# A selective-scan kernel: the first tap of its depthwise convolution on ScalarE instead of VectorE

## The reference, cut to what matters

```python
xr = x @ W_in
x_in, res = jnp.split(xr, 2, axis=-1)
xc = jnp.transpose(x_in, (0, 2, 1))
xc = lax.conv_general_dilated(xc, conv_w, (1,), [(d_conv - 1, 0)], feature_group_count=d_inner)
xc = xc + conv_b[None, :, None]
u = jax.nn.silu(jnp.transpose(xc, (0, 2, 1)))
...
def step(h, inp):
    u_t, d_t, B_t, C_t = inp
    h = jnp.exp(d_t[..., None] * A) * h + (d_t * u_t)[..., None] * B_t[:, None, :]
    y = jnp.einsum('bds,bs->bd', h, C_t)
    return (h, y)
...
y = y * jax.nn.silu(res)
return y @ W_out
```

## Time and profile before

| | before |
|---|---|
| median of three runs | 2191.8 us (2189.04 to 2195.35) |
| the profiled execution | 2192.7 us, of which span 2190.9 us |
| PE busy | 2052.0 us (94%) |
| DVE busy | 1500.5 us (68%) |
| POOL busy | 1484.7 us (68%) |
| ACT busy | 1450.1 us (66%) |
| largest shares of the last chain | PE 55%, DVE 15%, ACT 14% |

### The profile page before, as it was taken

One profiled execution on the slowest core, in us unless ns is written; L12 is line 12 of the kernel. 1 busy time (PEld: TensorE's weight loads), 2 busy tenths in 40 slices (PEclk: granted clock), 3 DMA queues, 4 the chain that ended last, 5 costly groups with the idle time before them and its releaser, 6 DMA issues.

```text
span 2190.9 us, 30857 instructions
## 1 busy us (share of the span) xinstructions
PE 2052.0 (94%) x11952; PEld 1444.5 (66%) x11952; DVE 1500.5 (68%) x1507; ACT 1450.1 (66%) x2294; POOL 1484.7 (68%) x845
## 2 busy tenths in 40 slices
PE   6989899999999999999999999999999889999997
PEld 3457677777777777777676777777777764444443
DVE  1268888888897989797879888887888970111201
ACT  0278888898887888888878888888788731000000
POOL 0039897989898888989897979798889960000000
PEclk9989999999999999999999999999999999989999
DMA  5211111111111112111111121111111410000000
GB/s 182 88 58 40 58 41 60 40 60 49 60 39 59 39 60 68 41 68 39 61 41 58 41 68 40 60 42 66 40 50 39 155 59 37 1 29 0 10 0 19
DMA packets 34137, 113.13 MB, mean 52 GB/s; under 512 B 6148, under 2 KB 8836, under 8 KB 33480
## 3 DMA queue, kind: packets, MB, share of 16 engines
q1 hardware_dynamic: 33992, 111.17, 14.9%
HBM read 95.95 MB, written 15.20 MB: 51 GB/s over the span
## 4 chain that ended last, share of the span: by engine, by line
PE 55%; DVE 15%; ACT 14%; issue 11%; POOL 4%; DMA 1%; SPq 0%; DVEq 0%; POOLq 0%; ACTq 0%
PE b_ps L1107 11%; PE y_all L1118 9%; DVE hid L855 8%; ACT hid L545 6%; ACT dub_t L558 5%; PE y_all L1216 5%; PE b_ps L1216 4%; DVE u L730 4%; PE bank_b L999 3%; POOL hid L418 3%; PE bank_a L1014 3%; PE y_all L919 3%; PE bank_b L1014 2%; PE bank_a L1023 2%; PE y_all L1229 2%
## 5 line engine op out<-in xcount | busy, mean ns | idle before, releaser
L855 DVE TENSOR_TENSOR_SCAN hid<-hid,b_ps 128x512 f32<-128x512 f32 x1024 | 1213.5, 1209 | 247.6 <-PE b_ps L1107 225.9
L418 POOL TENSOR_TENSOR hid<-hid,c_rep 128x1024 f32<-128x1024 f32 x512 | 1208.3, 2388 | 200.1 <-DVE hid L855 200.1
L1107 PEld LDWEIGHTS b_ps<-ident,dub_t 128*128 128x128 f32 x4096 | 481.8, 143 | 389.3 <-issue 220.1
L1107 PE MATMUL b_ps<-ident,dub_t 128*128 128x128 f32 x4096 | 637.8, 279 | 71.2 <-DVE hid L855 67.1
L545 ACT ACTIVATE hid<-delta,neg_a 128x512 f32<-128x512 f32 x1024 | 652.9, 711 | 0.4
L1118 PE MATMUL y_all<-ident,hid 128*128 128x128 f32 x4096 | 619.9, 275 | 7.3 <-POOL hid L418 6.3
L558 ACT ACTIVATE dub_t<-du_t,b_t 128x512 f32<-128x512 f32 x768 | 490.3, 712 | 58.9 <-PE b_ps L1107 57.2
L1118 PEld LDWEIGHTS y_all<-ident,hid 128*128 128x128 f32 x4096 | 484.1, 142 | 11.1 <-POOL hid L418 11.1
L409 POOL TENSOR_SCALAR dub_t<-du_t,b_t 128x512 f32<-128x512 f32 x256 | 174.7, 710 | 0.0
L730 DVE SCALAR_TENSOR_TENSOR u<-bank_b,conv_w_sb,u 128x511 f32<-128x511 f32 (+2 forms) x192 | 139.3, 725 | 0.7
L999 PE MATMUL bank_b<-xn,w_in_sb 128*128 128x512 f32 x256 | 132.1, 602 | 3.3 <-DVE u L730 3.3
(11 more groups left out here) (190 smaller groups left out, 1783.2 us busy)
## 6 DMA issues: line engine op xcount, KB each, us to landing
c_rep<-bc_dram SPq DMA_DIRECT2D x128, 512.0 KB, 3.7
hid<-x_t SPq DMA_DIRECT2D x4, 2048.0 KB, 8.7
x_dram<-x_out SPq DMA_DIRECT2D x16, 512.0 KB, 2.9
xt<-x_dram SPq DMA_DIRECT2D x15, 512.0 KB, 3.7
h_dram<-hid SPq DMA_DIRECT2D x4, 512.0 KB, 3.3
out<-y_d SPq DMA_DIRECT2D x4, 512.0 KB, 2.6
x_dram<-hid SPq DMA_DIRECT2D x3, 512.0 KB, 2.7
c_rep<-x_dram SPq DMA_DIRECT2D x3, 512.0 KB, 5.1
```

The source lines that it names most:

```text
L418: nc.gpsimd.tensor_tensor(part, part, c_rep[:, n % 2, s % GROUP, :].unsqueeze(1) .broadcast_to([P, HALF, SEQ]), ALU.mult).then_inc(hc_read ...
L855: nc.vector.tensor_tensor_scan(hid[:, i % RING, d, :], hid[:, i % RING, d, :], b_ps[d % 2][:, :], 0.0, ALU.mult, ALU.add)\
L1107: last = nc.tensor.transpose(b_ps[d % 2][:, c * P:(c + 1) * P], dub_t[:, i % DUB, c, d * P:(d + 1) * P], ident[:, :])
```

## The change

Tap 0 leaves DVE. ACT makes it with one activation (Identity, scale and bias each a column of 128 values) from `bank_b`, behind the same two waits that DVE had. In ACT's program it stands behind `decay` of s = 10, 12 and 14 for tiles 0, 1, 2 of block k+2, and behind `decay` of s = 0 of the next iteration for tile 3. DVE keeps taps 1 to 3 at their steps, and they still count on `conv[m]`.

```diff
+                    def first_tap(k, m):
+                        act.wait_ge(x_done, NI * k + m + 1)
+                        if k >= 2:
+                            act.wait_ge(skip_done, NI * (k - 2) + m + 1)
+                        nc.scalar.activation(u[:, k % 2, m, :], bank_b[:, :], ACT.Identity, scale=conv_w_sb[:, m, CONV - 1:CONV],
+                                             bias=vec_sb[:, 0, m:m + 1]).then_inc(conv[m], 1)
+
...
                             if live(k):
                                 decay(k, s)
+                            if s in (10, 12, 14) and live(k + 2):
+                                first_tap(k + 2, (s - 10) // 2)
+                            if s == 0 and live(k + 1):
+                                first_tap(k + 1, NI - 1)
...
                     def tap(k, m, t):
-                        if t == 0:
-                            dve.wait_ge(x_done, NI * k + m + 1)
-                            if k >= 2:
-                                dve.wait_ge(skip_done, NI * (k - 2) + m + 1)
-                            nc.vector.tensor_scalar(u[:, k % 2, m, :], bank_b[:, :], conv_w_sb[:, m, CONV - 1:CONV],
-                                                    vec_sb[:, 0, m:m + 1], ALU.mult, ALU.add).then_inc(conv[m], 1)
...
-                    TAP_AT = {(9, 2): (0, 0), (9, 3): (0, 1), (10, 0): (0, 2), (10, 1): (0, 3),
...
+                    TAP_AT = {(9, 3): (0, 1), (10, 0): (0, 2), (10, 1): (0, 3),
```

More of the change, by code:

```diff
@@ L720, in tap @@
                     def tap(k, m, t):
-                        if t == 0:
-                            dve.wait_ge(x_done, NI * k + m + 1)
-                            if k >= 2:
-                                dve.wait_ge(skip_done, NI * (k - 2) + m + 1)
-                            nc.vector.tensor_scalar(u[:, k % 2, m, :], bank_b[:, :], conv_w_sb[:, m, CONV - 1:CONV],
-                                                    vec_sb[:, 0, m:m + 1], ALU.mult, ALU.add).then_inc(conv[m], 1)
[L727 to L731, removed]
+                        w = CONV - 1 - t
+                        dve.wait_ge(conv[m], CONV * k + t)
+                        nc.vector.scalar_tensor_tensor(u[:, k % 2, m, t:], bank_b[:, 0:SEQ - t], conv_w_sb[:, m, w:w + 1],
+                                                       u[:, k % 2, m, t:], ALU.mult, ALU.add).then_inc(conv[m], 1)
                     def b_copy(k):
@@ L744, in gating @@
                                                 gate_t[:, k % 2, :, dc * P:(dc + 1) * P], ALU.mult).then_inc(gated, 1)
-                    TAP_AT = {(9, 2): (0, 0), (9, 3): (0, 1), (10, 0): (0, 2), (10, 1): (0, 3),
[3 rows of a table removed]
+                    TAP_AT = {(9, 3): (0, 1), (10, 0): (0, 2), (10, 1): (0, 3),
+                              (11, 3): (1, 1), (12, 0): (1, 2), (12, 1): (1, 3),
+                              (13, 3): (2, 1), (14, 0): (2, 2), (14, 1): (2, 3),
+                              (15, 3): (3, 1)}
                     LATE_TAP_AT = {(0, 0): (3, 2), (0, 1): (3, 3)}
```

## The result

| | before | after |
|---|---|---|
| median | 2191.5 us (4 runs, 2189.0 to 2195.4) | 2249.0 us (4 runs, 2241.0 to 2252.4) |
| ratio, 95% interval | | 1.0256 (1.0223 to 1.0288) |
| the profiled execution | 2192.7 us, span 2190.9 | 2251.4 us, span 2249.6 |
| mean granted TensorE clock | 0.977 of full speed | 0.961 |

Slower, as predicted, but by 57.5 us where 20 were forecast and 32 was the end of the range. The prediction's mechanism is in the trace; so is something else, more than half of the loss, that it had waved through.

What follows compares the result with a forecast made beforehand. It took waits between evenly loaded engines as the bound, chiefly PE waiting for ACT's gate at s = 4. 1.35 us for each of 15 iterations, 20.2 us, gave 2212.0 us; range 2197 to 2224, 8 in 10.

Steps and rivals of the forecast that it cites:

- The mechanism: ACT, running in order, waits at first taps for `in_x` and holds up what follows; 1.35 us per iteration lost.
- its four places: First taps of tiles 0 to 3 on ACT, with idle times near 2.7, 3.7, 1.5 and 1.6 us.
- Rival 1: The gain as meant: ACT's spare time hides the added passes, 19 us gained, 2173 us; chance 0.07.
- Rival 2: Tile 3's delay holds, copies held at (9,2), (11,2), (12,2) are absorbed: -0.14 us per iteration, 2190 us; chance 0.09.
- The sum: From gate to gate, 1.35 us lost per iteration, over 15 iterations 20.2 us.
- steps A to C: Tiles 0 to 2: late taps hold copies that PE waits for, leaving tile 3's `in_x` 0.34 us late.
- step D: Tile 3's tap: `times_b` 1 starts 3.97 us late against 2.3 us spare; gate 0 ends 1.35 us late.
- A: Tile 0's tap delays `y_copy` 3, holding PE's `du_turn` 0 by 0.6 us; 0.53 gained becomes 0.13 lost.
- C: At (12,2), `out_x` waits for `du_copy` 3; behind DVE's three taps PE is 0.45 us late.
- B: Tile 1's tap delays `du_copy` 2, holding PE's `du_turn` 3; the scan of (11,3) starts 0.30 us late.
- I take these to cancel: First iteration: smaller loss at tile 0 without `y_copy`, against tile 3's tap coming later in warm-up; no net size.
- One iteration stands for all: Iteration 8 was read for all; they repeat to hundredths of a microsecond, apart from the first and last two.

Runs made afterwards that it cites:

- e5: The changed kernel with all four first taps moved later in ACT's order, to where ACT reaches them after PE's bank is full: 2186.6 us, ratio 0.9973.
- e1: The changed kernel with tile 3's first tap given back to DVE, tiles 0, 1, 2 staying on ACT: 2219.5 us, ratio 1.0134.
- e2: The kernel before with only tile 3's first tap moved to ACT: 2221.5 us, ratio 1.0141.
- e12: The changed kernel with 18 extra 128-column transposes among PE's narrow products and 16 at the gate: 2237.3 us, ratio 1.0205 to the kernel before.
- e11: The kernel before with 18 extra 128-column transposes among PE's narrow products and 7 at the gate: 2214.5 us, ratio 1.0101.
- e8: The changed kernel with 18 extra 128-column transposes mixed into PE's narrow products, none added at the gate: 2258.6 us, ratio 1.0288.
- e4: The changed kernel with 16 extra transposes on PE ahead of the product that waits for gate 0: 2230.7 us, ratio 1.0181.
- e3: The kernel before, no tap moved, with six small unused ACT passes ahead of gate 0 to delay it: 2227.9 us, ratio 1.0176.
- e10: The kernel before with first taps of tiles 0 and 1 on ACT at later places, and `decay` 4 ahead of `times_b` 4: 2161.2 us, ratio 0.9845.

## Why the prediction was wrong in size, step by step

**Right.** The mechanism, its four places and its sign. ACT's idle times at tiles 0 to 3 were forecast as 2.7, 3.7, 1.5 and 1.6 and are 2.64, 3.80, 1.58 and 1.54; PE was to wait at `du_turn` 0 and does, 0.57 us; the pass was to take 0.78 and takes 0.777; `times_b` 4 no longer waits; PE's wait for the gate went to 2.33 by its weight load (forecast 2.5); no table load was added. Rival 1, the gain as meant, needed 3.97 us of spare time and fell; e5 shows that it would have been right with other places. Rival 2, D alone, fell too: e1 shows 0.58 us for A to C, not a gain.

**A term sized a little low.** The sum was 1.35 us per iteration and the undisturbed iteration grew by 1.57. The 0.22 are all in steps A to C: tile 3's `in_x` was to be 0.34 late, and e1 puts that shift at 0.58; step D by itself was 1.35 - 0.34 = 1.01, and e2 measured 1.01. The traces show where. Starts behind the gate, in an iteration at full clock (gate at 986.22 in before, at 700.02 in after):

| | before | after | later by | forecast |
|---|---|---|---|---|
| `du_turn` 0 | 43.28 | 44.02 | 0.74 | 0.6 |
| `in_x` of tile 1 | 54.67 | 54.93 | 0.26 | 0.13 |
| `du_turn` 3 | 56.41 | 57.31 | 0.90 | 0.77 |
| `out_x` of (12,2) | 62.04 | 62.78 | 0.74 | 0.51 |
| `in_x` of tile 3 | 80.07 | 80.66 | 0.59 | 0.34 |

About half of the missing time comes in at A and half at C, none at B. At both PE starts 0.14 us or so behind the end of the copy that it waits for (1072.25 + 0.59 to 1072.98 above), where I had reckoned 0.04 and 0.05. Over 15 iterations the 0.22 are 3 us. (One small slip beside it: by the prediction's own range, 4.5 us for 0.07 us more of the pass, a pass of 799 ns would have added about 1.2 us, not under 1; it took 777.)

**A term left out.** "I take these to cancel", for the start of the program: gate 1 came 5.7 us late. e1, with tile 3's tap on DVE, has it at 164.1 us and e2 at 161.5, against 158.8, so it is mostly the taps of tiles 0 to 2; half-clock stretches before gate 1 are in it (23.9 us of them in after, 20.5 in before), and e12 is 3.1 us later there than e11.

**The step that failed.** "One iteration stands for all, since they repeat to within hundredths of a microsecond". They do when undisturbed. But in the trace of before three of the 14 were 4.6 to 4.9 us longer than the others, with the granted clock at half for 10.2 us. I had read a window at full clock and let the span's mean of 0.977 pass. The sum held those three fixed, and gave the clock only the 4 us by which the range's ends were widened, taken from the spread of three runs. In fact their number changes with the program: 3 in before, 9 in after with 3 short ones, and the 32 us that this cost are more than the 20 of the forecast. With the clock held equal (e11, e12) the forecast was 20.2 us and the result 22.8.

**What stays open.** With wide products mixed into the narrow ones no long stretch is left in 42 iterations of three kernels (e8, e11, e12), while each of the ten kernels without them had 2 to 9 in 14. The mixed-in products also make the iteration 2.57 us longer, and no run added that time at this place without wide products, so that their width does it is likely, not shown. For the short ones it is idle time at the gate (e4, e12). But the narrow products are the same in every kernel and in every iteration, and only some iterations are hit. The hits have an order: in before every fourth iteration, in e1 every second, in after three of four. So it does not look like chance, and the order differs between kernels whose iterations differ by 0.6 to 1.6 us; what picks them is not shown here. Most edits raised the number, one that made the iteration shorter (e5, 6) as well as one that made it longer (e3, 7); e10 stayed at 3 and e2 has 2 beside its nine short ones. One profile each does not tell the count's scatter either; by their times, runs of before differ by some 15 us, about three long stretches.

## What to carry to other kernels

Placing work on an engine with spare time costs by where it stands in that engine's order: three passes of 0.68 us in front of copies that PE waits for cost 0.6 us per iteration together, a single one in front of the gates cost 1.0, and the same four passes a few instructions later gained 1.24. Before one iteration is taken for all, list the lengths of all of them with their granted clock; if some are longer at half clock, what a change does to their number is a term of the sum, with a range from none to every iteration (here 14 x 4.55 us, about 64 us). To judge a change by itself, compare it on a version of both kernels in which PE is kept at full clock; then 22.8 us was seen with a scatter under 4 us, where the plain kernels gave 57.5.

## What the runs showed of the hardware

TensorE's granted clock fell to half while the profile had PE busy without a gap, at products 1 and 16 columns wide; with 18 transposes of 128 columns mixed in, none of 42 iterations of three kernels had such a long stretch. A long one (10.2 us) cost 4.55 us of time, one of 13.7 us some 6.2, and a short one (3.4 us) behind an idle PE 1.7, both from the length of the iterations. With an idle time of 2.10 us at the gate some iterations had a short one; filled down to 0.23 (e4, e12) none had. Sixteen transposes in PE's idle time, with results that nobody reads, made the kernel 18 us faster.
